# Spreading the operations of a small table among VectorE's other work of one pipeline step

## What is computed

```python
# x, ctx_1024: (32, 128, 256)
x = x + tanh(g_xattn[0]) * xattn(layernorm(x), ctx_1024, ctx_1024, ...)
x = x + tanh(g_ffn[0]) * ffn(layernorm(x), router_w, w1, b1, w2, b2)

# xattn: causal softmax attention of 16 heads, q/k/v/out projections with biases
# ffn:
logits = x @ router_w
assignments = argmax(logits, -1)
weights = softmax(logits)[assignments]
hid = gelu(x @ w1[e] + b1[e])           # e: the token's expert
moe_out = (hid @ w2[e] + b2[e]) * weights
```

## Time and profile before

| | |
|---|---|
| median of three executions | 518.8 us |
| the profiled execution: time, span | 518.15 us, 516.3 us |
| TensorE busy (matmuls) | 479.1 us, 93% |
| VectorE busy | 334.4 us, 65% |
| ScalarE busy | 320.5 us, 62% |
| GpSimd busy | 271.5 us, 53% |
| TensorE's mean granted clock | 0.981 |

### The profile page before, as it was taken

The page is one execution under the profiler, slowest core; times in us unless marked ns, Lnnn a source line. Parts: engine busy times, 40 slices in busy tenths (PEclk is TensorE's granted clock), DMA queues, the critical chain, the costliest instruction groups (busy, mean ns, idle before and its releaser), DMA issues.

```text
span 516.3 us, 16821 instructions
## 1 busy us (share of the span) xinstructions
PE 479.1 (93%) x4898; PEld 415.4 (80%) x4899; DVE 334.4 (65%) x1066; ACT 320.5 (62%) x1456; POOL 271.5 (53%) x502
## 2 busy tenths in 40 slices
PE   4789999999999999999999997978989999999991
PEld 3578888888888888888888877867889999999981
DVE  3577798888888888888898875652334334343421
ACT  1789899897898888889889866350233232323230
POOL 3553536456456456455555636465545655555621
PEclk9999999999999999999999988997999999999997
DMA  6354554112112121122111039486879888888800
GB/s 209 99 168 153 190 181 153 46 52 74 52 50 62 51 71 41 51 71 51 56 55 41 2 109 271 157 211 192 272 229 263 284 270 273 274 282 263 272 29 1
DMA packets 37480, 72.69 MB, mean 141 GB/s; under 512 B 12601, under 2 KB 21055, under 8 KB 37440
## 3 DMA queue, kind: packets, MB, share of 16 engines
q1 hardware_dynamic: 24480, 31.87, 20.8%
q10 hardware_dynamic: 5904, 23.54, 14.2%
q0 software_dynamic: 7056, 16.79, 10.3%
HBM read 58.80 MB, written 15.07 MB: 143 GB/s over the span
## 4 chain that ended last, share of the span: by engine, by line
PE 35%; ACT 30%; DVE 14%; issue 10%; DMA 4%; POOL 4%; another core or an unknown queue 1%; DVEq 1%; ACTq 0%; POOLq 0%
ACT arena L681 28%; PE bank L1193 14%; PE bank L1183 13%; DVE negmax L872 3%; DMA g_rows<-token_rows,fetch_idx 3%; PE bank L1170 2%; PE bank L1283 2%; DVE stats L979 2%; ACT arena L725 2%; POOL token_names L479 1%; PE bank L1224 1%; PE bank L1232 1%; DVE moments L1064 1%; DVE moments L985 1%
## 5 line engine op out<-in xcount | busy, mean ns | idle before, releaser
L681 ACT ACTIVATE arena<-bank,negmax 128x128 f32<-128x128 f32 x512 | 181.8, 401 | 41.9 <-DVE negmax L872 41.9
L665 ACT ACTIVATE hid_t<-bank,w_ring 128x128 f32<-128x128 f32 x180 | 51.2, 368 | 117.4 <-PE bank L1183 91.2
L681 ACT ACTIVATION_READ_ACCUMULATOR arena<-bank,negmax 128x1 f32 x512 | 123.2, 241 | 0.0
L1193 PE MATMUL bank<-W,hid_t 128*128 x360 | 88.0, 388 | 3.7 <-DVE g_out L861 1.7
L1183 PE MATMUL bank<-g_xt,w_ring 128*128 128x128 f32 x720 | 88.9, 277 | 2.2 <-DVE g_xt L845 2.1
L1183 PEld LDWEIGHTS bank<-g_xt,w_ring 128*128 128x128 f32 x720 | 85.4, 193 | 3.6 <-issue 3.2
L872 DVE TENSOR_REDUCE negmax<-bank 128x4 f32<-128x512 f32 x128 | 84.0, 678 | 6.2 <-PE bank L1216 4.7
L488 POOL TENSOR_TENSOR arena<-arena,C 128x256 f32<-128x256 f32 x64 | 37.8, 610 | 88.9 <-ACT arena L725 88.9
L1224 PE MATMUL bank<-C,arena 128*128 128x128 f32 x512 | 79.9, 279 | 4.6 <-ACT arena L681 3.3
L861 DVE SCALAR_TENSOR_TENSOR g_out<-bank,g_name,g_out 128x256 f32<-128x256 f32 x45 | 21.8, 484 | 88.1 <-PE bank L1193 79.8
L1193 PEld LDWEIGHTS bank<-W,hid_t 128*128 128x128 f32 x360 | 66.3, 195 | 12.7 <-issue 5.2
(11 more groups left out here) (122 smaller groups left out, 713.6 us busy)
## 6 DMA issues: line engine op xcount, KB each, us to landing
w_ring<-w1b ACTq DMA_DIRECT2D x35, 642.0 KB
token_rows<-rows SPq DMA_DIRECT2D x32, 256.0 KB, 2.3
W<-w SPq DMA_DIRECT2D x14, 512.0 KB
w_ring<-w1b SPq DMA_DIRECT2D x10, 642.0 KB
arena<-x SPq DMA_DIRECT2D x32, 128.0 KB, 2.1
arena<-ctxt SPq DMA_DIRECT2D x31, 128.0 KB, 2.1
slot_names<-token_names SPq DMA_DIRECT2D x45, 1.0 KB
g_rows<-token_rows,fetch_idx POOLq DMA_INDIRECT x45
```

Of the source, the lines that this page charges most:

```text
L665: ins = act.activation(hid_t[:, RING[k], ch, :], hid_bank[k][:, ch * P:(ch + 1) * P], ACT.Gelu, bias=w_ring[:, k, B1_AT + ch:B1_AT + ch + 1])
L681: ins = act.activation(probs[:, q, v, :], bank[q][:, v * P:(v + 1) * P], ACT.Exp, bias=negmax[:, b.par, h:h + 1], accum_out=rsum[:, b.par, ...
L1193: ins = pe.matmul(bank[4][:, 0:D], hid_t[:, RING[r], ch, :], W2[:, bass.ds(ex, 1), ch, :].rearrange("p e n -> p (e n)"), start=(ch == 0), ...
```

## The change

The first operation on the counts stays in its place. The nine others, which stood in a row at the end of step 32, are put one or two at a time between VectorE's operations of the same step. Each still waits for `table_step`, now raised by an operation that lies several others back. The order of `t_key` and `t_past` is swapped, and `slot_columns` is raised by an instruction of its own behind the last one.

```diff
-            def full_tiles():
-
-                link(dve.tensor_scalar(t_tiles, t_tiles, ROUND, -ROUND, ALU.add, ALU.add))
-                place(const("next_region"))
+            def early_tiles(stage):
+
+                if stage > 1:
+                    dve.wait_ge(table_step, stage - 1)
+                if stage == 1:
+                    ins = dve.tensor_scalar(t_tiles, bank[5][:, COUNT:COUNT + E], (1 - P) / 2.0, 1.0 / P,
+                                            ALU.add, ALU.mult)
+                if stage == 2:
+                    ins = dve.tensor_scalar(t_tiles, t_tiles, ROUND, -ROUND, ALU.add, ALU.add)
+                if stage == 3:
+                    ins = dve.tensor_tensor_scan(t_cum, t_one, t_tiles, 0.0, ALU.mult, ALU.add)
+                if stage == 4:
+                    dve.tensor_scalar(t_past, t_cum, index, None, ALU.is_le)
+                    ins = dve.scalar_tensor_tensor(t_key, t_cum, float(-P), const("next_region"), ALU.mult, ALU.add)
+                if stage == 5:
+                    ins = dve.tensor_tensor(t_at[:, 1:E + 1], t_key, t_past, ALU.mult)
+                if stage == 6:
+                    dve.tensor_reduce(t_e, t_past, axis=AX_X, op=ALU.add)
+                    ins = dve.tensor_reduce(t_c, t_at, axis=AX_X, op=ALU.max)
+                if stage == 7:
+                    dve.tensor_scalar(t_row, index, float(P), t_c, ALU.mult, ALU.add)
+                    ins = dve.tensor_scalar(t_e, t_e, float(E - 1), None, ALU.min)
+                ins.then_inc(table_step, 1)
+                if stage == 7:
+                    dve.sem_inc(slot_columns, 1)
+                done[0] = stage
...
                     if t.static and t.n == 32:
-                        dve.tensor_scalar(t_tiles, bank[5][:, COUNT:COUNT + E], (1 - P) / 2.0, 1.0 / P, ALU.add, ALU.mult)
+                        early_tiles(1)
...
                     transposed_probs(b, 0)
+                if t.static and t.n == 32:
+                    early_tiles(2)
                 if h.ok():
                     normed_rows(h)
+                if t.static and t.n == 32:
+                    early_tiles(3)
...
+                if t.static and t.n == 32:
+                    early_tiles(4)
                 if b.ok():
                     maxima(b, 3)
+                if t.static and t.n == 32:
+                    early_tiles(5)
                 if c.ok():
 
                     residual(c)
+                if t.static and t.n == 32:
+                    early_tiles(6)
                 if b.ok():
                     transposed_probs(b, 1)
                     reciprocal(b)
+                if t.static and t.n == 32:
+                    early_tiles(7)
...
-                if t.static and t.n == 32:
-                    full_tiles()
```

## The result

Ten executions of the changed kernel took 516.62 us in the median (515.86 to 517.89), ten of the kernel before, in the same comparison, 519.79 us (517.12 to 522.44). The ratio is 0.9947, with a 95% interval of 0.9923 to 0.9972: 1.5 to 4.0 us less. A second comparison gave 0.9948 (0.9917 to 0.9979). The prediction said 2.0 us less than the profiled execution, 516.2 us, within a range of 514.0 to 519.0.

The account below looks back on a forecast made before the run. It took VectorE's row ending step 32, holding up ScalarE and TensorE, as the bound there. VectorE's 1.3 us, inside TensorE's 2.6, left 2.0 us at the end: 518.15 - 2.0 = 516.15, 516.2 us, range 514.0 to 519.0.

Parts of the forecast that it names:

- The row lies on the path in full: End of step 32 on VectorE: nothing needed runs beside the small table operations, so 1.68 us leaves the path.
- 0.08 us for a moved operation: VectorE, step 32: each moved operation costs 0.08 us in its new place, since its wait is long fulfilled.
- The rival in which small operations cost their full length: VectorE: about 0.165 us per operation wherever it stands, 0.2 us gained there, 517.2 us at the end; chance 0.03.
- The price of 0.21 us: VectorE's row: an operation starts 0.21 us after the one it reads; high bound for a moved operation, leaving 0.6 us gained.
- What the places delay: Step 32: query delayed at no cost, ScalarE's exponentials and reciprocal 0.2 us late, choice and statistics 0.4 us; VectorE nets 1.3 us.
- TensorE keeps its clock: Step 33: without the 1.23 us wait the clock stays full; 2.6 us gained in all, VectorE's 1.3 us inside it.
- The table 1.3 us earlier: Behind VectorE's normalised attention in step 33: table copy, load of names and weight loads come 1.3 us earlier.
- Two limits behind the first gather: Engines' chain 2.6 us earlier competes with full transfers begun 1.3 us earlier; the middle, 2.0 us, reaches the end.
- The first row of the slots without a gap: Sign, where TensorE becomes busy without a gap: this row comes 1.3 to 2.6 us earlier.
- The collision: Rival: the first gather follows 1.3 us closer behind the weight loads and slows, a second likewise; 520.6 us, chance 0.08.
- if the gathers take over 8 us: Sign, gathers on GpSimd and the DMA queues: such a duration would show the forecast wrong.
- The gain is used up: Rival: gathers and name scatters set the pace from 309 us on, waiting for full transfers; 518.2 us, chance 0.14.

Follow-up runs that it names:

- dummy_row: Changed kernel plus nine chained operations that nobody reads at the end of step 32, where the table's row stood; ratio 1.0002 to the kernel before.
- fill_short: Kernel before plus 4 unread 128x96 matmuls on TensorE ahead of the two table lines of step 33; ratio 0.9996 to the kernel before.
- before_gather: Kernel before with the third gather on GpSimd ahead of the name scatters of batches 24 and 25; ratio 0.9964 to the kernel before.
- table_early: Changed kernel with the table's lines made on TensorE at the end of step 32 and copied behind VectorE's statistics; ratio 0.9945 to the kernel before.
- table_late: Changed kernel with SyncE also waiting for the query of step 33 before loading the first names; ratio 0.9965 to the kernel before.
- gather_early: Changed kernel with the third gather on GpSimd ahead of the name scatters of batches 24 and 25; ratio 0.9910 to the kernel before.
- fill_gap: Kernel before plus 12 unread 128x96 matmuls on TensorE ahead of the two table lines of step 33; ratio 1.0046 to the kernel before.
- changed again: The changed kernel unaltered, run in a second comparison against the kernel before; ratio 0.9948.
- lines_late: Kernel before with the table's two lines made on TensorE behind step 33's product of attention and values, in another bank; ratio 0.9993 to the kernel before.

## Why the prediction was right, step by step

- **The row lies on the path in full**: right. dummy_row puts such a row back, and the gain goes.
- **0.08 us for a moved operation**: right. The nine take 0.72 us together, 0.08 each. The rival in which small operations cost their full length is out: VectorE gained 1.22 us, not 0.2. The Trainium skill, VectorE: DVE Perf Modes, "The DRAIN you can't avoid", says that a semaphore between operations costs nothing extra, from a measurement of `tensor_copy`. Here it does: the same nine take 1.68 to 2.13 us in a row and 0.72 us spread. The same section says that a next operation which is not held starts earlier; the prediction left that sentence out, and the starts 0.07 us apart agree with it. The price of 0.21 us was misread as that of reading a result: `t_past` at 296.72 does not read the `t_key` ahead of it, it waits for its semaphore. And not every operation of the row goes through `link`; the sum `t_e` doesn't, and the next one starts 0.08 us behind it even in the row:

```profile
297.19 0.17 DVE L807 TENSOR_REDUCE t_e<-t_past 128x1 f32<-128x14 f32 x1
297.27 0.16 DVE L808 TENSOR_REDUCE t_c<-t_at 128x1 f32<-128x15 f32 x1
297.47 0.22 DVE L809 TENSOR_SCALAR t_row<-C,t_c 128x1 f32<-128x1 f32 x1
```

- **What the places delay**: right in place, a little small. The query cost nothing. The fourth maximum held ScalarE up by 0.28 us (0.2 forecast), the reciprocal came 0.21 us late. VectorE's net was 1.22 us, 1.3 forecast. ScalarE's wait ahead of its first exponential of step 33 is 0.74 us, 1.0 forecast.
- **TensorE keeps its clock**: right, shown by fill_short. The sum of 2.6 us was too large; it measured 2.25. The term that I put at nothing is the rank sums and the lines, which step 33 has ahead of its transposes and step 32 has not: from the logits to the next transposes of reciprocals it takes 0.82 us in step 33 and 0.50 in step 32. I had taken step 32's 2.85 us for both. The rule of the Trainium skill, TensorE: Matmul & The Clock Gate, "What's actually happening", that the clock follows how busy the engine has lately been, agrees with the traces: from 298 to 302 the clock is 0.64 (before) and 0.57 (before_gather) behind the 1.23 us wait in the two kernels that have it, 1.00 in the other twelve traces, where that wait is 0.26 us at most. The length of a wait alone doesn't tell whether the clock falls: 1.00 follows 1.59 us in dummy_row, 2.09 in the changed kernel and 2.46 in table_early (ahead of the first gather's rows), and 0.50 (312 to 315) follows 1.88 us in before_gather.
- **The table 1.3 us earlier**: 1.1 us, because VectorE waits 0.27 us for TensorE's `mixed_done` ahead of its copy. It turned out not to matter.
- **Two limits behind the first gather**: this step was argued wrongly, though the number came out well. I held that full transfer queues would tie the third gather to the start of the weight loads, and so allowed only half of the difference between 1.3 and 2.6 us to pass. It took 8.7 us before and after, though it was issued 2.3 us earlier; table_early and table_late move the loads and hardly the end; gather_early moves the issue by 2.7 us and the rows are used 3.1 us earlier (behind the counts). So the place in GpSimd's list is what moved this gather. That the loads have no part in it is not shown: the 7.1 us of table_late speak for some part.
- **At the end** 2.8 us by the first ratio, 2.7 by the second, against 2.0: inside the intervals, and nearer to the 2.25 us of step 33 and the 2.3 us of the third gather than to my middle. That 516.2 lies so close to the measured 516.62 is in part luck: the kernel before took 519.79 us in this comparison, 1.6 more than the profiled execution from which I subtracted, and the gain was larger than forecast; the two nearly cancel. The first row of the slots without a gap was to come 1.3 to 2.6 us earlier; in the pair of traces it is 0.9 us. And I held 5.2 us to be the least that can be told from none: the intervals here are 1.3 to 1.6 us either way, and they tell 2.8 us.
- The collision did not come (5.74 us for the first gather, issued 2.7 us earlier behind the counts). The sign "if the gathers take over 8 us" was badly put: the third took 8.7 us, but it had before. "The gain is used up" is refuted by both intervals.

Three things stay open: how much TensorE's kept clock is worth by itself at the end, why fill_gap lost 2.4 us, and why the single traces of before and after differ by only 0.9 us where the medians of ten differ by 3.2. The traces show that the clock falls in other places in each execution (0.69 from 345 to 350 before, 1.00 there after), which fits, but no run tests it. Part of it is which executions were profiled: the one before took 1.6 us less than its median, the one after 0.6 us more.

## What to carry to other kernels

Here small operations that wait for one another cost 0.19 to 0.25 us each in a row, and 0.08 us each between larger ones, where the semaphore was up already: look for such a row at the end of a step, where two engines wait for what comes behind it. Count what the place that you move them to delays, and compare two steps only after the work that one has and the other lacks is listed. And when a gain shifts an engine forward, look at once for its next wait: here one swap on GpSimd, worth 2.0 us more by the middle values (0.9910 against 0.9948), was visible in the trace as a wait of 2.39 us.

## What was not expected of the hardware

- A matmul of 128x96 in f32 is two records of 0.12 us: 24 took 2.90 us, 8 took 1.11. My filler was sized as if it were one.
- The row of table operations took 1.68 us in one place and 2.13 us in another, most of the difference in the scan (0.59 us to the next start in place of 0.22).
- The third indirect gather of 128 rows of 2 KB took 8.7, 8.7, 9.1, 9.0 and 9.0 us to where TensorE, waiting, used its rows (before, changed, changed again, lines_late, fill_gap), whether issued at 312 or 315 us, but 8.0 us in table_early and 7.1 in table_late.
